# Two-layer message-passing network on one core: code for unusual inputs moved from the main loops to each layer's end, and node chunks asked for half as often

## The reference

```python
h = jnp.maximum(_layernorm(x, axis=-1), 0.0)

def _dmpnn_layer(x, src, dst, edge_attr, W_msg, Wih, Whh, bih, bhh):
    msg = jnp.concatenate([x[src], edge_attr], axis=-1) @ W_msg.T
    agg = jax.ops.segment_sum(msg, dst, num_segments=n_nodes)
    return _gru_cell(agg, x, Wih, Whh, bih, bhh)

h = layer1(h); h = layer2(h)
out = x + h
```

## Time and profile before

| | us |
|---|---|
| Median of three runs (3688.25 to 3702.47) | 3693.58 |
| The profiled execution, its own time | 3698.19 |
| Its span in the profile | 3696.4 |
| PE busy in it | 2875.1 (78%) |
| POOL busy in it | 2479.5 (67%) |
| DVE busy in it | 1493.4 (40%) |
| ACT busy in it | 1004.8 (27%) |
| Mean granted TensorE clock | 0.803 |

### The profile page before, as it was taken

The page is one execution under the profiler, slowest core; times in us unless marked ns, Lnnn a source line. Parts: engine busy times, 40 slices in busy tenths (PEclk is TensorE's granted clock), DMA queues, the critical chain, the costliest instruction groups (busy, mean ns, idle before and its releaser), DMA issues.

```text
span 3696.4 us, 82116 instructions
## 1 busy us (share of the span) xinstructions
PE 2875.1 (78%) x20436; PEld 2565.0 (69%) x20437; DVE 1493.4 (40%) x4420; ACT 1004.8 (27%) x2006; POOL 2479.5 (67%) x2528
## 2 busy tenths in 40 slices
PE   1887988898898888888876777777877787787786
PEld 1776877787787686777756667666766676676675
DVE  6444444444444443434332334333433443343342
ACT  5122222222232322232331222222322232232232
POOL 2777777776776675756607777777777766676661
PEclk9887988887887887887876768777877877887887
DMA  7333333333333232323315222222222222222221
GB/s 173 85 86 83 95 86 87 86 87 75 84 88 79 74 84 68 87 68 74 79 26 115 56 59 57 59 60 60 62 59 62 62 56 57 61 58 54 60 55 28
DMA packets 371230, 267.78 MB, mean 72 GB/s; under 512 B 240088, under 2 KB 330016, under 8 KB 370472
## 3 DMA queue, kind: packets, MB, share of 16 engines
q0 software_dynamic: 80128, 164.07, 17.7%
q1 hardware_dynamic: 266086, 71.80, 9.7%
q10 hardware_dynamic: 24258, 22.75, 2.2%
HBM read 239.14 MB, written 19.20 MB: 70 GB/s over the span
## 4 chain that ended last, share of the span: by engine, by line
PE 54%; issue 17%; DVE 7%; POOL 7%; DVEq 7%; ACT 4%; ACTq 2%; DMA 2%; POOLq 0%; SPq 0%
PE ps_v L614 16%; PE ps_win L657 13%; POOL rows L532 7%; PE ps_win L640 6%; PE ps_c L607 3%; PE ps_q L607 3%; DVEq L992 3%; PE ps_a L737 2%; DVEq L960 2%; PE ps_c L739 2%; PE ps_c L741 2%; ACTq L1223 1%; PE ps_b L742 1%; PE ps_d L744 1%; PE ps_d L746 1%
## 5 line engine op out<-in xcount | busy, mean ns | idle before, releaser
L532 POOL DMA_INDIRECT rows<-h_table,idx x1252 | 1229.5, 982 | 598.9 <-issue 394.8
L532 POOL DMA_INDIRECT rows<-x_table,idx x1252 | 1228.6, 981 | 522.0 <-issue 426.8
L657 PE MATMUL ps_win<-onehot,rows 128*128 128x80 f32 x5008 | 844.7, 321 | 295.4 <-issue 279.7
L657 PEld LDWEIGHTS ps_win<-onehot,rows 128*128 128x128 f32 x5008 | 745.7, 228 | 371.8 <-issue 359.6
L614 PE MATMUL ps_v<-hr,a_blk 125*120 125x128 f32 x5200 | 809.4, 328 | 0.0
L614 PEld LDWEIGHTS ps_v<-hr,a_blk 125*120 125x120 f32 x5200 | 789.5, 236 | 0.0
L1186 ACT COPY a_blk<-ps_q 125x390 f32<-125x390 f32 (+1 forms) x416 | 220.7, 530 | 1243.7 <-PE ps_q L607 1120.2
L927 DVE SCALAR_TENSOR_TENSOR v_hot<-v_cur,lane 128x390 bf16<-128x390 f32 (+1 forms) x834 | 422.7, 544 | 0.0
L640 PE MATMUL ps_win<-onehot,attr 128*64 128x80 f32 x3128 | 340.3, 264 | 104.2 <-issue 80.6
L1001 DVE TENSOR_TENSOR aggT<-aggT,ps_win 128x80 f32 x626 | 144.2, 230 | 661.3 <-PE ps_win L657 539.6
L640 PEld LDWEIGHTS ps_win<-onehot,attr 128*64 128x64 f32 x3128 | 280.4, 157 | 143.1 <-issue 99.8
(11 more groups left out here) (161 smaller groups left out, 2027.3 us busy)
## 6 DMA issues: line engine op xcount, KB each, us to landing
attr<-in_edge_attr_dram SPq DMA_DIRECT2D x390, 128.0 KB
rows<-h_table,idx POOLq DMA_INDIRECT x1252
rows<-x_table,idx POOLq DMA_INDIRECT x1252
dst_in<-in_dst_dram SPq DMA_DIRECT2D x702, 2.0 KB
idx<-in_src_dram SPq DMA_DIRECT2D x624, 2.0 KB
x_table<-out_sb ACTq DMA_DIRECT2D x50, 125.0 KB
attr<-in_x_dram ACTq DMA_DIRECT2D x50, 125.0 KB
out_dram<-out_sb ACTq DMA_DIRECT2D x50, 125.0 KB
```

The costliest lines, as they stand in the source:

```text
L532: nc.gpsimd.indirect_dma_start(out=rows[0:parts, s, j, :], out_offset=None, in_=table[:, :], in_offset=bass.IndirectOffsetOnAxis(ap=idx[0: ...
L657: mm = nc.tensor.matmul(ps_win[r % 2][:, 0:WIN], rows[0:parts, rr, j, :], onehot[0:parts, r % 2, j, :], start=(j == 0), stop=(j == TILES - 1))
```

## The change

It takes `extra_windows` and `again` out of the loops on PE, DVE and ACT. In their place stands `overflow`, once at each layer's end before `last_chunks`, on all five engines: it loads one flag, `over_i`, and if that is set, loads, gathers and sums the affected groups and blocks again. The branch on `window_wide` goes too; such blocks are treated in `overflow`. DVE's setup at the start computes the flag, and, where it is set, makes no chunk ready before the layer's end; for that the last operations of the `ready_i` table are moved behind the flag. `ready_chunks` is asked after gathered group 11 and at the iteration's end alone, and looks two steps back. The core of the diff:

```diff
         def ready_chunks(eng, step, chunk):
-            low = eng.value_load(ready_i[0:1, bass.ds(step, 1)], min_val=0, max_val=CHUNKS)
+            low = eng.value_load(ready_i[0:1, bass.ds(step - 1, 1)], min_val=0, max_val=CHUNKS)
             high = eng.value_load(ready_i[0:1, bass.ds(step + 1, 1)], min_val=0, max_val=CHUNKS)
+        def overflow(eng, body):
+            any_over = eng.value_load(over_i[0:1, 0:1], min_val=0, max_val=1)
+            with eng.If(any_over > 0):
+                body()
 # PE, group and attr_group
                     pe.wait_ge(rows_loaded[rr], rows_n * (16 * TILES) + 16 * TILES)
-                    extra_windows(r, rr, g, parts, True)
                     for j in range(TILES):
                         mm = nc.tensor.matmul(ps_win[r % 2][:, 0:WIN], rows[0:parts, rr, j, :],
 # PE, the loop and behind it
                         if last:
                             window_of_block(blk)
-                            again(it, blk)
-                        if last or (gi is not None and gi % RING == RING - 1 and gi + 1 < SLOTS):
+                        if last or gi == SLOTS // 2 - 1:
                             u = SUBS - 1 if last else gi // RING
                             ready_chunks(pe, it * SUBS + u,
...
+                overflow(pe, over_body)
                 last_chunks(pe, lambda i: chunk(i, ORDERED[0] + layer * ORDERED[1], (layer + 1) * ITERS,
 # DVE, setup
+            nc.vector.tensor_copy(tm_b, tm[:, :].unsqueeze(2).to_broadcast([TROWS, TCOLS, VC]))
...
+            chained(nc.vector.tensor_reduce(over[:, 1:2], v_bad[:, :], AX.X, ALU.max))
+            nc.vector.tensor_copy(npass_i, v_pass[0:1, :])
+            chained(nc.vector.tensor_tensor(over[:, 0:1], over[:, 0:1], over[:, 1:2], ALU.max))
+            nc.vector.tensor_copy(over_i, over[0:1, 0:1])
+            chained(nc.vector.tensor_scalar(over_need[:, :], over[:, 0:1], float(STEPS + 1), None, ALU.mult))
+            chained(nc.vector.tensor_tensor(need[0:VC, :], need[0:VC, :], over_need[:, :], ALU.max))
+            nc.vector.tensor_scalar(bend[0:VC, :], bend[0:VC, :], need[0:VC, 0:1], None, ALU.is_ge).then_inc(need_ready, 1)
 # DVE, loop
                     base = dve.value_load(base_i[0:1, bass.ds(g, 1)], min_val=0, max_val=N)
-                    extra_windows(p, s, g, parts, base, sent)
                     added_before(p)
...
-                    wide = dve.value_load(window_wide[0:1, bass.ds(it, 1)], min_val=0, max_val=1)
                     at = dve.value_load(window_base[0:1, bass.ds(it, 1)], min_val=0, max_val=N)
...
+                added_before(TAIL[layer] + 1)
+                overflow(dve, over_body)
                 last_chunks(dve, chunk)
```

More of the change, by code:

```diff
@@ L485, in _ @@
                     sp.dma_start(dst_in[0:REST, r, :], edges(dst, FULL, REST)).then_inc(dst_loaded[r], 16)
+                overflow(sp, lambda: over_body(layer))
         @block.gpsimd
@@ L554, in _, with over_gather @@
                 gather(0, 0, REST)
+                def over_gather(g, parts, sent, n, done):
+                    pool.wait_ge(over_idx, done * 16 + 16)
+                    pool.sem_inc(gather_issued, 1)
+                    for j in range(TILES):
+                        nc.gpsimd.indirect_dma_start(
+                            out=rows[0:parts, 0, j, :], out_offset=None, in_=table[:, :],
+                            in_offset=bass.IndirectOffsetOnAxis(ap=idx[0:parts, 0, 0, j:j + 1].bitcast(U32), axis=0),
+                        ).then_inc(over_rows, 16)
+                overflow(pool, lambda: over_groups(pool, over_count, over_gather))
         @block.tensor
@@ L578, in _ @@
                 nc.tensor.matmul(ps_d[0:VC, at], tb_b[:, k, :], turn, start=True, stop=True)
-                mm = nc.tensor.matmul(ps_v[0:1, at], tm[:, k:k + 1], turn, start=True, stop=True)
+                mm = nc.tensor.matmul(ps_v[0:VC, at], tm_b[:, k, :], turn, start=True, stop=True)
             mm.then_inc(tiles_turned, 1)
@@ L618, in _ @@
             for layer in range(2):
[L619 to L636, removed]
@@ new lines, in over_group @@
+                def over_group(g, parts, sent, n, done):
+                    pe.wait_ge(over_attr, done * 16 + 16)
+                    pe.wait_ge(over_rows, done * (16 * TILES) + 16 * TILES)
+                    pe.sem_inc(over_seen, 1)
+                    with pe.Fori(0, n):
+                        pe.reg_add(extra_count, extra_count, 1)
+                        count = pe.snap(extra_count, min_val=1, max_val=1 << 20)
+                        pe.wait_ge(x_onehot_ready, count)
+                        for j in range(TILES):
+                            nc.tensor.matmul(ps_win[0][:, XAT:XAT + XWIN], rows[0:parts, 0, j, :],
+                                             onehot_x[0:parts, j, :], start=(j == 0), stop=(j == TILES - 1))
+                        for j in range(TILES):
+                            mx = nc.tensor.matmul(ps_win[0][0:D, XAT + XWIN:XAT + 2 * XWIN], attr[0:parts, 1, j, :],
+                                                  onehot_x[0:parts, j, :], start=(j == 0), stop=(j == TILES - 1))
+                        mx.then_inc(x_summed, 1)
+                        pe.wait_ge(x_added, count)
@@ L645, in hot_wait, with group @@
                     pe.wait_ge(onehot_ready, p + (layer * (ORDERED[0] + 1) + 1))
[L647 removed]
+                def group(p, r, rr, parts, attr_n, rows_n):
                     if layer == 0:
@@ L689, in window_of_block @@
                                      start=True, stop=True).then_inc(v_summed, 1)
[L691 to L710, removed]
-                            pe.reg_add(again_count, again_count, 1)
@@ new lines, in over_block @@
+                def over_block(it, n):
+                    with pe.Fori(0, n):
+                        passed = pe.snap(again_count, min_val=0, max_val=1 << 16)
+                        for sl in range(SLICES):
+                            for k in range(PACKS):
+                                i = sl * PACKS + k
+                                pe.wait_ge(again_hot, passed * (SLICES * PACKS) + (i + 1))
+                                if i > 1:
+                                    pe.wait_ge(again_kept, passed * (SLICES * PACKS) + (i - 1))
+                                build_pack(sl, k).then_inc(again_built, 1)
+                            pe.wait_ge(again_kept, passed * (SLICES * PACKS) + (sl + 1) * PACKS)
+                            multiply(sl).then_inc(again_slice, 1)
+                        pe.wait_ge(again_acc, passed + 1)
+                        nc.tensor.matmul(ps_v[:, 256:256 + VC], v_rows[:, :], ident[0:VC, 0:VC],
+                                         start=True, stop=True).then_inc(again_turned, 1)
+                        pe.wait_ge(again_added, passed + 1)
+                        pe.reg_add(again_count, again_count, 1)
@@ L1066, in add_nodes, with over_body @@
+                def over_body():
+                    over_groups(dve, over_count, over_group)
+                    over_blocks(dve, over_block)
+                    for k in range(2):
+                        lo_pack(ITERS, k)
+                        ins = v_pack(v_cur, 0, k)
+                    ins.then_inc(over_restored, 1)
                 def add_nodes(cc):
```

248 lines of the change are left out of this document (147 added, 101 removed).

## The result

The changed kernel takes 3577.15 us (median of 4 runs, 3562.89 to 3585.51), the kernel before beside it 3693.39: ratio 0.9679, interval 0.9637 to 0.972. That is 116 us less; I forecast 3608, 85 less. The profiled execution took 3585.51 us, its span is 3583.8.

What follows compares the result with a forecast made beforehand. It took gathers to set a floor of 122.6 us per iteration and only time where PE is late above it as winnable. Layer 0 -80, layer 1 -8, setup +3 give -85 us: 3608 us, range 3545 to 3660.

Steps and rivals of the forecast that it cites:

- -80, -8 and +3: Sum by place: layer 0 80 us faster, layer 1 8 us faster, once-per-kernel setup 3 us slower.
- The branch over `again`: PE, iteration's end in layer 0: removing the long skip at L694 saves 3.8 us per iteration.
- the stall stays: Rival, 0.13: PE stalls because its code arrives late, so the 3.8 us turn up elsewhere; 3656 us.
- `extra_windows` on PE: Load, branch and register steps before every group on PE: removal saves 3 us per layer 0 iteration, bounds 0 and 4.
- `extra_windows` on DVE: Load and register steps before every window: removal saves 1.5 us per layer 0 iteration, only where PE waits for DVE.
- Half the asks: Taking chunks at two asks per iteration instead of four saves about 1 us per layer 0 iteration.
- Layer 1, -8: Layer 1 gains 8 us: 15 won in its last five iterations, some 7 lost in three earlier ones.
- the ring argument: Layer 1: long PE stops outlast POOL's six slots; that idle adds to the floor, 14.5 us where there were 17.4.
- an overflow: Rival, 0.05: longer stops at iteration ends idle POOL; layer 1 loses 29 us if PE's relief is hidden; 3724 us.
- The loop of layer 1 is kept: Rival, 0.05: layer 1's loop stays in PE's memory, so L748's 3.6 us vanish, 18 us in all; 3590 us.
- The clock comes back: Rival, 0.14: the 1.2 GHz stretch behind the iteration's end gap vanishes, 17 us per iteration; 3520 us.
- What would show it: Signs in the profile: branches over 1 us, gap near 6 us, layer 0's last six iterations 139 to 141, POOL idle near 19.

Runs made afterwards that it cites:

- four asks: The changed kernel with chunk readiness asked four times per iteration, as before the change, instead of twice: 3476.76 us, 0.9417 of the kernel before.

## Why the prediction was right, and where only its sum was

**The sign and the size came out; the working did not carry them.** I forecast -85 as -80, -8 and +3. Measured by the profiles it is -83.2, -30.8 and +1.4 in the same places. But layer 0's agreement is luck, two errors that cancel: moving the code gives 141 us there (four asks against before), and half the asks take 57 back.

- *The branch over `again`, -3.8*: right. The gap shrank by 4.5 in front of a chunk, and from 10.15 to 5.03 at an end without one (with four asks). The helper alone is worth 33 us against 38. So the rival *the stall stays*, 0.13, did not happen: the only branches of over 1 us on PE are twelve back in layer 0 and one for each layer.
- *`extra_windows` on PE, 3*: right in size. Alone it is worth 28, over ten iterations 2.8 each. But with VectorE unchanged PE waits for the one-hots instead, 166.4 us for 97.7.
- *`extra_windows` on DVE, 1.5, bounds 0 and 2.6*: the term that failed. It is worth 126 us. "DVE is under-used, so it counts only where PE waits for DVE" read its 97.7 us of waits as the ceiling of the gain. The busy share leaves out the sequencer, and the chain's DVEq 7% said 259 us. The upper bound was wrong as well: it allowed for the wait alone, not for the clock that goes with it.
- *Half the asks, -1*: wrong in sign and size. The working took a first chunk at 10.8 and a second at 11.4 from stretches before the change. In the kernel before these prices hold: half the asks give 7 us in the loop of layer 0 and cost 20 in that of layer 1. In the changed kernel the first costs 6.3, since it no longer loses the clock, and the second up to 14.6, and the loop of layer 0 loses 39. In both kernels two more chunks behind each loop add 39 or 40 us, for which I had no term.
- *Layer 1, -8*: the ring argument holds, its numbers do not. Half the asks cost 58 us there (profiles of four and two asks; 38 in the loop, 20 behind it), twice the 29 I gave to an overflow; the relief was 89, not the 8 + 29 = 37 that goes with it. "If layer 1 gains as much as layer 0, my ring argument has failed": it gained 0.37 as much. But the ring rules layer 0 too, where I had let PE alone set the time.
- *The loop of layer 1 is kept*, given 0.05: happened, and is worth 12 us of the 18 in its case. I had the rule and its number at hand and gave too little chance to a mechanism that the removal of hundreds of instructions plainly favoured.
- *The clock comes back*, 0.14: in part. An end stays at 0.63 to 0.75 in layer 0, its loop at 0.84 and that of layer 1 at 0.76 to 0.78, so the case as I wrote it did not happen. In layer 0 a stretch with one chunk mostly keeps 2.4 GHz, and the change has no such stretch left inside its last six iterations.
- *What would show it*: the last six iterations of layer 0 took 136.3 each, under my 139 to 141; the branches on PE were as listed, but for layer 1's, which are short. An end of layer 1 with three chunks leaves POOL idle 48.1 - 27.92 - 30 x 0.30 = 11, not 19.

## What to carry to other kernels

Price a deferred or merged step in the kernel as the rest of the change leaves it: a stop that has become short enough to keep the clock is cheap alone and dear in company. An engine's busy share says nothing about its sequencer; where the chain shows an engine's queue by name (DVEq), a register load per step is a candidate before any matmul is. And a change that does two things should be run as two: here one half was worth 216 us and the other cost 100. Count, too, what a deferred step leaves behind the last iteration, where nothing hides it: two chunks a layer were 39 us by the profiles.

## What the runs showed of the hardware

Code that is never run cost time once the loop outgrew what TensorE keeps. Eight bodies of 12 matmuls instead of one turned a branch of 0.22 us into one of 3.6 and the kernel 12 us slower, though the executed instructions are the same. Writing the loop out 13 times removed the branch back of layer 0 and brought no fetch stall that the time shows: -12.6 us, and 1.80 MB of code in q8 instead of 2.28.

VectorE's jump back does not show in its branch's own record (66 ns at L1104, median). It shows as 2.7 to 3.3 us before its next register instruction, 24 times in the trace before, and writing the loops out was worth 19 us. No run tells how much of the 19 is the jump and how much the clock that returned with it (0.71 to 0.84 in that stretch).
